# Low-rank attention on one core: 64-row products in pairs, and the sums of key tiles shared out anew

## Chip, core and metric

The kernel runs on one core of a Trainium2 chip. The metric is the device time of one execution in microseconds, median of several runs.

## What is computed

Six layers on x of shape 8 x 1024 x 128, each on the layer norm of the running sum: a low-rank expert layer, attention in windows of 64 with 16 heads, the expert layer again, a linear layer on values rounded to a 6-bit grid, low-rank attention, and the linear layer again. The change is in low-rank attention. Cut to what matters:

```python
# per batch b: y = layernorm(x[b]); y @ W_DKV, y @ W_KR, y @ W_DQ give 32 numbers each
q = concatenate([q_c, q_r], -1)             # 8 heads, 128 + 32
k = concatenate([k_c, k_r], -1)
scores = einsum('bhsd,bhtd->bhst', q, k) * scale
attn = softmax(scores, -1)                  # 1024 queries x 1024 keys
o = einsum('bhst,bhtd->bhsd', attn, v_c)
x = x + (o.transpose(...).reshape(...) @ W_O + b_O)
```

The products of weight matrices are taken beforehand, so that keys and queries of a head meet in 64 numbers (KR), the keys are the same for all heads of a batch, and values have 32 numbers (DC).

## The kernel before

There are 8 batches of 8 heads, 64 heads u in all, each with 8 key tiles of 128 keys (NT) and 1024 queries. A step g = 8u + t is one key tile of one head; 512 steps in all. For each engine the program runs over the same list of steps (`plan_m`, made by `low_rank_plan`), and each engine executes what it has in that order and waits on semaphores.

Precision is kept by splitting: keys and queries are held as a rounded high part and the low rest, both in a format that TensorE takes in one pass. `key_hl` has the high part in rows 0 to 63 and the low part in rows 64 to 127, `q_hi` has the high part of the queries twice, `key_h1` the high keys and a row of ones, `q_low` the low queries and a row with the shift of the exponent.

In step g TensorE (`pe_low_rank`) does, for each half of the columns:
- `pe_row_scores` (L1825) for a tile 14 steps ahead: 128 queries against 512 keys, one product of 128 rows. VectorE takes the maximum of each row (`dve_row_max`, L1833). When a head's maxima are there, `dve_row_top`, `pool_shift` and `sync_move_shift` make the shift of the exponent and move it by DMA into its row. The banks are 4, 5, 6 in turn (`ROW_BANKS`), shared with the totals;
- `pe_key_scores` (L1878 and L1882) for tile g: two products of 512 columns, 128 and 65 rows deep, into one bank. The banks are 0, 1, 2 in turn (`K_BANKS`), so half n waits for the exponential of half n - 3. ScalarE takes the exponentials (`act_exponentials`, L1893) into `prob1`, which has room for eight tiles.

Then come the low-rank items that the plan has put there (`pe_low_part`: queries of a later head, and once a batch the turned input, keys, constants, values, output projection and the last linear layer), which share bank 7: an item waits until the one before it in the bank has been taken away. On odd groups of four steps (g mod 8 = 3) and even ones (g mod 8 = 7) follows `pe_weigh`: four tiles are weighed with the values (L1936, 32 rows of output at four column places), and for g mod 8 = 3 the totals of a head are made first (L1929). For the totals GpSimd has added up tiles 0 to 6 of the head (`pool_sum`, L1904 and L1907), and TensorE adds that sum and tile 7. VectorE inverts the totals (`dve_invert_totals`, L1946) and scales the result (`dve_normalise`), and SP moves it (`sync_move_head`).

A wait stands in each engine's own program ahead of the instruction that needs it, and everything behind it on that engine stands too.

Of the kernel before, what the change touches and what calls it, by code (L numbers as in the profile page):

```python
# [225 lines left out]
PIPELINE = 16  # L226
# [3 lines left out]
def low_rank_plan():  # L230
# [34 lines left out]
    while g < NT * U + 26 or running or waiting:  # L265
        early, late = [], []
# [7 lines left out]
        if r == (12 if b < B else 7) and 1 <= b <= B:  # L274
            waiting[0:0] = [("proj", b - 1, i) for i in range(2)]
# [11 lines left out]
        if item is None and waiting and (g % 2 == 0 or g >= NT * U):  # L287
            item = waiting.pop(0)
        if item:
            run = begin(item, FINAL_BANKS.get((item[0], item[2]), 7) if item[1] == B - 1 else 7)  # L290
            late.append((tuple(run[:3]), 1))
            running.append(run)
        steps.append((g, early, late))
# [4 lines left out]
def build_program(nc, x_in, w128, w_mla, w_out_window, w33, w1, consts, out):  # L298
    ctx = ExitStack()
    with ctx:  # L300
# [37 lines left out]
        both_parts = sb("both_parts", [P, DC], F32R)  # L338
# [71 lines left out]
        w_query = sb("w_query", [QR + 2, NH, 2 * KR], F32R, low)  # L410
# [6 lines left out]
        key_hl = sb("key_hl", [P, 2, T], F32R, low)  # L417
        key_h1 = sb("key_h1", [KR + 1, 2, T], F32R, low)
# [3 lines left out]
        q_hi = sb("q_hi", [P, Q_BUFS, T], F32R, low)  # L422
        q_low = sb("q_low", [KR + 1, Q_BUFS, T], F32R, low)
        amax1 = sb("amax", [P, 2, NT, 2], F32, low)
        shift = sb("shift", [P, 2, 2, 4], F32, low)
        shift_cols = sb("shift_cols", [P, 2, 4], F32R, low)
# [1009 lines left out]
        def pool_layers(e):  # L1436
            for i in range(B + 1):
# [5 lines left out]
                if i == 3:  # L1443
                    e.wait_ge(*dequant.at(("c", i - 2)))
                    e.memset(key_h1[KR:KR + 1, :, :].bitcast(F32), 1.0).then_inc(*set_low.up("key row"))
                    e.wait_ge(*set_low.at("key row"))
# [30 lines left out]
        key_h1_done = signal("key_high_copied")  # L1477
# [5 lines left out]
        shift_moved = [(new_sem(f"shift_row_{k}_first_half"), new_sem(f"shift_row_{k}_last_half")) for k in range(Q_BUFS)]  # L1483

        def shift_ready(u, i):
            return shift_moved[u % Q_BUFS][i], 64 * (u // Q_BUFS + 1)
# [145 lines left out]
        def pe_low_part(e, item, j, before, part):  # L1632
# [5 lines left out]
            if kind == "query":  # L1638
                b, h = divmod(a, NH)
                e.wait_ge(*cq_ready.at((b, 1)))  # L1640
                e.matmul(bank(j), w_query[:, h, :], cq[:, b % 2, sl], start=True, stop=True,  # L1641
# [41 lines left out]
            else:  # L1683
                e.wait_ge(*mla_built.at("both"))
                e.wait_ge(*keys_done.at((a, 1)))
                for t in range(NT):
# [572 lines left out]
```

## Time and profile before

| | us |
|---|---|
| median of 3 runs | 1807.89 |
| lowest, highest | 1807.46, 1809.03 |
| span of the profiled execution | 1812.5 |
| TensorE busy | 1670.4 (92%) |
| VectorE busy | 1393.8 (77%) |
| GpSimd busy | 1177.3 (65%) |
| ScalarE busy | 1137.5 (63%) |
| mean granted TensorE clock | 0.967 |

The profiled execution is its own run; its time is taken here as its span, 4.6 us above the median. The layers before low-rank attention fill the first third of the span; the low-rank stage runs from about 610 to 1780 us. In it the profile shows few names: key and row products, exponentials, row maxima, sums, totals and weighing. Busy time on TensorE counts overlapping records once, and a product's record is longer than its share of the engine, since the next one starts before it ends.

### The profile page before, as it was taken

The numbers are of one execution on the slowest core, as the hardware profiler recorded it, in microseconds if no ns is written. First come the engines' busy times: TensorE is split into PE (matmuls) and PEld (weight loads), VectorE is DVE, ScalarE is ACT, GpSimd is POOL, SyncE is SP. The second block draws the span as 40 slices with busy tenths as digits, with TensorE's granted clock in tenths as the row PEclk, the third lists the DMA queues.
The fourth block names the chain that finished last, engine by engine and source line by source line (L and its number), as shares of the span: only waits on it lengthen the run. The fifth ranks groups of instructions, "written<-read, shape, count | busy, mean of one in ns | idle before, by whom it ended". The sixth has DMA issues, their size and how long they took to land.

```text
span 1812.5 us, 39662 instructions
## 1 busy us (share of the span) xinstructions
PE 1670.4 (92%) x15057; PEld 1223.0 (67%) x15057; DVE 1393.8 (77%) x2976; ACT 1137.5 (63%) x2222; POOL 1177.3 (65%) x909
## 2 busy tenths in 40 slices
PE   4679999999877899999999999999999999999995
PEld 4557777777766567666766766766676677677674
DVE  5557777766597888878888888888887888888862
ACT  5447777777676466666666666666656666665662
POOL 4300111000066498898898988989889898898892
PEclk9889999999887899999999999999999999999997
DMA  4556666654000000000000000001001000100101
GB/s 123 136 140 156 162 156 159 164 136 116 29 1 1 1 10 8 10 8 10 7 13 16 10 8 19 11 7 22 7 10 19 8 10 7 22 7 10 19 10 30
DMA packets 198677, 81.47 MB, mean 45 GB/s; under 512 B 152553, under 2 KB 177493, under 8 KB 198357
## 3 DMA queue, kind: packets, MB, share of 16 engines
q1 hardware_dynamic: 198484, 78.93, 19.5%
q8 instruction: 119, 1.95, 0.5%
q14 instruction: 74, 0.60, 0.1%
HBM read 39.79 MB, written 29.88 MB: 38 GB/s over the span
## 4 chain that ended last, share of the span: by engine, by line
PE 54%; DVE 11%; POOL 2%; issue 1%; ACT 1%; DMA 0%; SPq 0%; POOLq 0%; ACTq 0%
PE pair L1825 12%; PE pair L1878 11%; PE pair L1882 11%; PE pair L1936 10%; DVE amax L1833 4%; PE pair L1929 4%; PE pair L1650 2%; DVE o_inv L1946 1%; PE pair L1641 1%; DVE stats L485 1%; POOL w_mix L1907 1%; PE pair L1664 1%; DVE q_low L1754 1%; DVE cq L1765 1%; DVE key_hl L1768 1%
## 5 line engine op out<-in xcount | busy, mean ns | idle before, releaser
L1893 ACT ACTIVATE prob<-pair 128x512 f32<-128x512 f32 x1024 | 604.4, 597 | 422.2 <-PE pair L1882 359.6
L1833 DVE TENSOR_REDUCE amax<-pair 128x1 f32<-128x512 f32 x1024 | 670.3, 682 | 133.9 <-PE pair L1825 131.8
L1825 PE MATMUL pair<-key_hl,q_hi 128*128 128x512 f32 x1024 | 437.8, 430 | 11.2 <-DVE amax L1833 7.1
L1878 PE MATMUL pair<-q_hi,key_hl 128*128 128x512 f32 x1024 | 405.2, 396 | 2.6 <-ACT prob L1893 2.6
L1882 PE MATMUL pair<-q_low,key_h 65*128 65x512 f32 x1024 | 406.0, 396 | 0.0
L1907 POOL TENSOR_TENSOR w_mix<-w_mix,prob 128x1024 f32<-128x1024 f32 x160 | 382.3, 2389 | 25.2 <-ACT prob L1893 8.5
L1907 POOL TENSOR_TENSOR Wm<-Wm,prob 128x1024 f32<-128x1024 f32 x155 | 369.6, 2384 | 20.8 <-ACT prob L1893 4.1
L520 POOL TENSOR_SCALAR veps<-mv 128x8 f32<-128x8 f32 x47 | 11.4, 243 | 452.6 <-DVE mv L493 451.2
L1825 PEld LDWEIGHTS pair<-key_hl,q_hi 128*128 128x128 f32 x1024 | 196.1, 192 | 115.9 <-issue 51.0
L1936 PE MATMUL pair<-prob,values 128*32 128x256 f32 x4096 | 247.2, 382 | 0.0
L1186 DVE TENSOR_REDUCE mx_neg<-pair 128x4 f32<-128x512 f32 x256 | 164.9, 687 | 94.8 <-PE pair L1090 94.1
L1878 PEld LDWEIGHTS pair<-q_hi,key_hl 128*128 128x128 f32 x1024 | 195.5, 191 | 44.3 <-ACT prob L1893 9.4
L1882 PEld LDWEIGHTS pair<-q_low,key_h 65*128 65x128 f32 x1024 | 192.5, 188 | 44.6
L1936 PEld LDWEIGHTS pair<-prob,values 128*32 128x32 f32 x4096 | 127.5, 110 | 100.9 <-issue 25.0
L1136 ACT ACTIVATE yT<-pair 128x512 f32<-128x512 f32 x256 | 138.6, 593 | 72.3 <-PE pair L1042 70.3
L1946 DVE RECIPROCAL o_inv<-pair 128x256 f32<-128x256 f32 x64 | 112.5, 1758 | 59.8 <-PE pair L1929 59.8
L542 ACT ACTIVATE y<-x,mean_neg,rstd 128x128 f32<-128x128 f32 x336 | 137.7, 485 | 19.0 <-POOL mean_neg L528 18.9
L1090 PE MATMUL pair<-keys,queries 64*128 64x128 f32 x1024 | 100.5, 317 | 0.0
L1042 PE MATMUL pair<-queries,keys 64*128 64x128 f32 x1024 | 97.0, 309 | 0.0
L1702 ACT ACTIVATE q_hi<-pair 128x512 fp32r<-128x512 f32 x128 | 75.7, 591 | 20.0 <-PE pair L1641 20.0
L1754 DVE TENSOR_TENSOR q_low<-pair,q_hi 64x512 fp32r<-64x512 f32 x128 | 86.3, 675 | 2.2 <-ACT q_hi L1702 2.2
L1090 PEld LDWEIGHTS pair<-keys,queries 64*128 64x128 f32 x1024 | 82.7, 199 | 3.7
(209 smaller groups left out, 2232.8 us busy)
## 6 DMA issues: line engine op xcount, KB each, us to landing
rows_mem<-once SPq DMA_DIRECT2D x128, 128.0 KB, 2.0
queries<-rows_mem SPq DMA_DIRECT2D x64, 256.0 KB, 4.5
keys<-rows_mem SPq DMA_DIRECT2D x16, 1024.0 KB, 7.1
rows_mem<-once SPq DMA_DIRECT2D x128, 64.0 KB, 1.9
q_low<-shift_cols SPq DMA_DIRECT2D x512, 0.5 KB, 2.0
yT<-o_norm SPq DMA_DIRECT2D x256, 32.0 KB, 1.9
x<-x_dram SPq DMA_DIRECT2D x8, 512.0 KB, 7.3
out_dram<-x SPq DMA_DIRECT2D x7, 512.0 KB, 3.4
```

What stands on the lines that cost most here:

```text
L542: ins = e.activation(y_of(stage, b)[:, t, :], x[:, b * NT + t, :], ACT.Identity, bias=mean_neg[:, k, t:t + 1], scale=rstd[:, k, t:t + 1])
L1090: ins = e.matmul(bank(S_BANKS[r])[:, q * P:(q + 1) * P], queries[rows, hb % QUERY_BUFS, q, m].rearrange("p s w -> p (s w)"), keys[rows, b ...
L1136: e.activation(pT[:, u % P_TURNED].rearrange("p q k -> p (q k)"), key_row_bank(*divmod(u, 2)), ACT.Exp).then_inc(*exps.up(u))
L1186: e.tensor_reduce(mx_neg[:, hb % 2, r, :, m], bank(S_BANKS[r]).rearrange("p (q k) -> p q k", q=QUADS), AX_X, ALU.max, negate=True).then_in ...
L1825: e.matmul(row_bank(("row", r, i)), q_hi[:, k, t * P:(t + 1) * P], key_hl[:, b % 2, i * HALF:(i + 1) * HALF], start=True, stop=True, skip_ ...
L1833: e.tensor_reduce(amax1[:, u % 2, t, i:i + 1], row_bank(("row", r, i)), AX_X, ALU.max).then_inc(*row_maxed.up((r, i)))
L1878: e.matmul(bank(j), key_hl[:, b % 2, ks], q_hi[:, k, sl], start=True, stop=False, skip_group_check=True)
L1882: e.matmul(bank(j), key_h1[:, b % 2, ks], q_low[:, k, sl], start=False, stop=True, skip_group_check=True).then_inc(*key_scored.up((g, half)))
L1893: e.activation(prob1[:, g % P_BUFS, half * HALF:(half + 1) * HALF], bank(K_BANKS[(2 * g + half) % 3]), ACT.Exp, scale=SCALE1).then_inc(*ke ...
L1907: e.tensor_tensor(into, into, p, ALU.add).then_inc(*summed_keys.up(g))
L1936: ins = e.matmul(bank(PVB)[q * DC:(q + 1) * DC, 0:QUARTER], values[:, b % 2, t, :], prob1[:, g % P_BUFS, q * QUARTER:(q + 1) * QUARTER], s ...
L1946: e.reciprocal(o_inv[:, u % 2, :], row_bank(("total", u, 0))[:, 0:QUARTER]).then_inc(*o_inverse.up(u))
```

## The change

- Keys and queries: `key_high` has the high keys in rows 0 to 63 and again in 64 to 127, `key_low` the low keys twice. `q_hi` and `q_low` have the first 512 queries in rows 0 to 63 and the last 512 in rows 64 to 127, and so does the new `q_shift`, of which only rows 0 and 64 are not zero; `ones_shift` is all ones. A head's queries come from two products into one bank, then one copy and one subtraction of 128 rows.
- Row scores are made of the high parts alone, by two products of 64 rows, one in each half of the rows, into two banks.
- Key scores of a tile are four such pairs: high keys with high queries, low keys with high queries, high keys with low queries, ones with the shift. Both sides begin together, after the waits for both banks.
- GpSimd adds up six tiles of a head instead of seven; two go to the totals directly.
- The plan: the queries come at g mod 8 = 7, other items only at g mod 8 = 3, one ahead of the weighing and, unless it or the next is a key product (`low`), one behind it.
- The shift is made once a head and moved by eight DMAs in a row.

```diff
     def regular(g):
-        for i in range(2):
-            u, rest = divmod(g + 16 - 4 * i, NT)
-            if rest == 0 and 0 <= u < U:
-                return "query", u, i
-        return None
+        u, rest = divmod(g + PIPELINE, NT)
+        return ("query", u, 0) if rest == 0 and 0 <= u < U else None
...
-        if item is None and waiting and (g % 2 == 0 or g >= NT * U):
+        if item is None and waiting and (g % NT == 3 or g >= NT * U):
             item = waiting.pop(0)
...
+        if g % NT == 3 and 0 <= g < NT * U and waiting and item[0] != "low" and waiting[0][0] != "low":
+            run = begin(waiting.pop(0))
+            after.append((tuple(run[:3]), 1))
+            running.append(run)
...
-                e.matmul(bank(j), w_query[:, h, :], cq[:, b % 2, sl], start=True, stop=True,
+                e.matmul(bank(j), w_query[:, h, KR:3 * KR], cq[:, b % 2, 0:HALF], start=True, stop=False,
+                         skip_group_check=True)
+                e.matmul(bank(j), w_query[:, h, 0:2 * KR], cq[:, b % 2, HALF:T], start=False, stop=True,
                          skip_group_check=True).then_inc(*query_done.up((a, i)))
...
                 for t in range(NT):
-                    ins = e.matmul(bank(j)[:, t * DC:(t + 1) * DC], key_hl[:, a % 2, t * P:(t + 1) * P], both_parts[:, :],
-                                   start=True, stop=True, skip_group_check=True)
+                    for part in (key_high, key_low):
+                        ins = e.matmul(bank(j)[:, t * DC:(t + 1) * DC], part[:, a % 2, t * P:(t + 1) * P],
+                                       first_dims[:, :], start=part is key_high, stop=part is key_low,
+                                       skip_group_check=True)
...
+        def pe_row_scores(e, r):
+
+            u, t, half = row_tiles(r)
             b, k = u // NH, u % Q_BUFS
...
+            for side in range(2):
+                row_bank_free(e, ("row", r, side))
+            for side in range(2):
+                rows = slice(side * KR, (side + 1) * KR)
+                e.matmul(row_bank(("row", r, side)), q_hi[rows, k, t * P:(t + 1) * P],
+                         key_high[rows, b % 2, half * HALF:(half + 1) * HALF], start=True, stop=True,
+                         skip_group_check=True).then_inc(*row_scored.up((r, side)))
...
-            if n >= 3:
-                e.wait_ge(*key_exp.at(divmod(n - 3, 2)))
-            e.matmul(bank(j), key_hl[:, b % 2, ks], q_hi[:, k, sl], start=True, stop=False, skip_group_check=True)
...
+            banks = [bank(K_BANKS[(2 * g + side) % 3]) for side in range(2)]
...
+            for side in range(2):
+                if 2 * g + side >= 3:
+                    e.wait_ge(*key_exp.at(divmod(2 * g + side - 3, 2)))
+            for part in range(4):
...
+                for side in range(2):
+                    rows = slice(side * KR, (side + 1) * KR)
+                    weights = ones_shift[rows, :] if part == 3 else (key_low if part == 1 else key_high)[rows, b % 2, ks]
+                    moving = (q_hi, q_hi, q_low, q_shift)[part][rows, k, :]
+                    ins = e.matmul(banks[side], weights, moving, start=part == 0, stop=part == 3, skip_group_check=True)
+                    if part == 3:
+                        ins.then_inc(*key_scored.up((g, side)))
...
                 if u < B * NH - 1:
-                    e.wait_ge(*summed_keys.at(NT * u + 6))
-                    parts = prob1[:, (NT * u + 7) % P_BUFS, :], key_sum[u % 2]
+                    e.wait_ge(*summed_keys.at(NT * u + 5))
+                    parts = *(prob1[:, (NT * u + t) % P_BUFS, :] for t in (6, 7)), key_sum[u % 2]
...
-                for half in range(2):
-                    if 0 <= g + ROW_LEAD < total:
-                        pe_row_scores(e, g + ROW_LEAD, half)
-                    if 0 <= g < total:
-                        pe_key_scores(e, g, half)
+                if 0 <= g + ROW_LEAD < total:
+                    pe_row_scores(e, g + ROW_LEAD)
+                if 0 <= g < total:
+                    pe_key_scores(e, g)
                 for (item, j, before), part in late:
                     pe_low_part(e, item, j, before, part)
                 if g % 4 == 3 and 0 <= g // 4 - 1 < total // 4:
                     pe_weigh(e, g // 4 - 1)
+                for (item, j, before), part in after:
+                    pe_low_part(e, item, j, before, part)
...
-                if (g - 1) % NT in range(1, 7) and 0 <= g - 1 < total - NT:
+                if (g - 1) % NT in range(1, 6) and 0 <= g - 1 < total - NT:
                     pool_sum(e, g - 1)
```

## Rows read from the trace of the kernel before

**Rows 1.** Of the page, part 1: busy us of each engine (share), instructions.

```profile
PE 1670.4 (92%) x15057; PEld 1223.0 (67%) x15057; DVE 1393.8 (77%) x2976; ACT 1137.5 (63%) x2222; POOL 1177.3 (65%) x909
```

**Rows 2.** Stretch, length, busy of five engines, granted clock, DMA share, GB/s.

```profile
1200.00:1400.00 200.00, 195.57 (x1507) 137.23 (x1506) 166.35 (x310) 125.56 (x230) 179.97 (x126) 1.00 0.09 14
```

**Rows 3.** Timeline of one head: start us, duration, instruction [idle before].

```profile
1206.44 0.39 PE L1882 MATMUL pair<-q_low,key_h 65*128 65x512 f32 x1
...
1206.87 1.30 ACT L1893 ACTIVATE prob<-pair 128x512 f32<-128x512 f32 x2 [3.02 <-PE pair L1882]
...
1207.14 0.40 PE L1882 MATMUL pair<-q_low,key_h 65*128 65x512 f32 x1
```

**Rows 4.** The same timeline, totals and weighing after step 3 of a head.

```profile
1202.83 0.39 PE L1882 MATMUL pair<-q_low,key_h 65*128 65x512 f32 x1
...
1203.14 0.64 PE L1929 MATMUL pair<-prob,ones_col 128*32 128x256 f32 x8
...
1203.60 0.61 PE L1929 MATMUL pair<-Wm,ones_col 128*32 128x256 f32 x8
...
1205.87 0.19 PEld L1825 LDWEIGHTS pair<-key_hl,q_hi 128*128 128x128 f32 x1 [0.41 <-issue]
```

**Rows 5.** The same timeline, a wait for ScalarE and a weighing without totals.

```profile
1211.24 1.05 ACT L1893 ACTIVATE prob<-pair 128x512 f32<-128x512 f32 x2
...
1211.87 0.50 PE L1878 MATMUL pair<-q_hi,key_hl 128*128 128x512 f32 x1 [0.36 <-ACT prob L1893]
...
1212.21 0.40 PE L1882 MATMUL pair<-q_low,key_h 65*128 65x512 f32 x1
...
1214.40 0.50 PE L1825 MATMUL pair<-key_hl,q_hi 128*128 128x512 f32 x1
...
1215.67 0.40 PE L1882 MATMUL pair<-q_low,key_h 65*128 65x512 f32 x1
```

**Rows 6.** Timeline of TensorE in the window stage, with pairs of 64-row products.

```profile
301.87 0.39 PE L1085 MATMUL pair<-mask_bf,both_rows 64*128 64x512 bf16 x2 [0.17 <-DVE mx_neg L1186]
301.90 0.74 PE L1090 MATMUL pair<-keys,queries 64*128 64x128 f32 x8
302.49 0.39 PE L1035 MATMUL pair<-both_rows,mask_bf 64*128 64x512 bf16 x2
...
303.20 1.07 PE L1061 MATMUL pair<-yT,vals 128*17 128x128 f32 x32
```

**Rows 7.** Lines, 640 to 1740 us: xcount | busy, mean ns | idle.

```profile
L1833 DVE TENSOR_REDUCE amax<-pair 128x1 f32<-128x512 f32 x957 | 627.5, 682 | 123.4 <-PE pair L1825 121.3
L1893 ACT ACTIVATE prob<-pair 128x512 f32<-128x512 f32 x958 | 567.6, 597 | 391.3 <-PE pair L1882 330.8 <-POOL Wm L1904 6.1
...
L1907 POOL TENSOR_TENSOR w_mix<-w_mix,prob 128x1024 f32<-128x1024 f32 x150 | 358.5, 2390 | 23.9 <-ACT prob L1893 8.5
...
L1946 DVE RECIPROCAL o_inv<-pair 128x256 f32<-128x256 f32 x60 | 105.5, 1758 | 36.1 <-PE pair L1929 36.1
```

**Rows 8.** Timeline of TensorE in the last steps.

```profile
1769.82 0.74 PE L1929 MATMUL pair<-prob,ones_col 128*32 128x256 f32 x8 [1.76 <-POOL w_mix L1907]
```

**Rows 9.** Timeline of the head above, ScalarE normalising four tiles.

```profile
1209.70 1.63 ACT L542 ACTIVATE y<-x,mean_neg,rstd 128x128 f32<-128x128 f32 x4
```

**Rows 10.** Who waited for whom, 640 to 1740 us: total us, times, longest.

```profile
PEld pair L1825 <- DVE amax L1833: 14.0, 35, 1.3
...
PEld pair L1878 <- ACT prob L1893: 6.5, 13, 0.8
```

**Rows 11.** TensorE by stretch: stretch, length, busy, granted clock, DMA share, GB/s.

```profile
139.50:375.00 235.50, 220.37 (x3250) 0.99 0.63 155
603.80:613.90 10.10, 9.40 (x20) 0.54 0.06 0
```

**Rows 12.** Timeline of the first key tile, at the lower clock.

```profile
611.19 0.63 PE L1882 MATMUL pair<-q_low,key_h 65*128 65x512 f32 x1
...
611.62 0.63 PE L1825 MATMUL pair<-key_hl,q_hi 128*128 128x512 f32 x1
```

More of the change, by code:

```diff
@@ L225 @@
 ROW_LEAD = 14
-PIPELINE = 16
+PIPELINE = 17
 Q_BUFS, P_BUFS = 3, 8
@@ L265, in low_rank_plan @@
     while g < NT * U + 26 or running or waiting:
-        early, late = [], []
+        early, late, after = [], [], []
         b, r = divmod(g, NT * NH)
@@ L1801, in build_program @@
         row_uses = []
-        for g, early, late in plan_m:
+        for g, early, late, after in plan_m:
             if 0 <= g + ROW_LEAD < total:
@@ new lines, in dve_row_max, with dve_row_top @@
+        def dve_row_max(e, r, side):
+            u, t, half = row_tiles(r)
+            e.wait_ge(*row_scored.at((r, side)))
+            if u >= 2:
+                e.wait_ge(*row_topped.at(u - 2))
+            e.tensor_reduce(amax1[:, u % 2, NT // 2 * side + t, half:half + 1], row_bank(("row", r, side)), AX_X,
+                            ALU.max).then_inc(*row_maxed.up((r, side)))
+        def dve_row_top(e, u):
+            e.wait_ge(*row_maxed.at((NT * u + NT - 1, 1)))
+            if u:
+                e.wait_ge(*shift_steps.at((u - 1, 1)))
+            e.tensor_reduce(shift[:, 0, :], amax1[:, u % 2, :, :], AX_X, ALU.max).then_inc(*row_topped.up(u))
@@ new lines, in pool_shift @@
+        def pool_shift(e, u):
+            b, h = divmod(u, NH)
+            top, mc = (shift[:, n, :] for n in range(2))
+            c = ccol[:, b % 2, :, h]
+            e.wait_ge(*row_topped.at(u))
+            e.wait_ge(*const_ready.at(b))
+            if u:
+                e.wait_ge(*shift_steps.at((u - 1, 2)))
+            e.tensor_tensor(mc, top, c, ALU.add).then_inc(*shift_steps.up((u, 1)))
+            e.wait_ge(*shift_steps.at((u, 1)))
+            if u:
+                e.wait_ge(*shift_ready(u - 1))
+            e.tensor_tensor(shift_cols[:, :], c, mc, ALU.subtract).then_inc(*shift_steps.up((u, 2)))
@@ new lines, in sync_move_shift @@
+        def sync_move_shift(e, u):
+            e.wait_ge(*shift_steps.at((u, 2)))
+            queries_free(e, u)
+            if u == 0:
+                e.wait_ge(*set_low.at("shift rows"))
+            for t in range(NT):
+                side, n = divmod(t, NT // 2)
+                e.dma_start(q_shift[side * KR:side * KR + 1, u % Q_BUFS, n * P:(n + 1) * P].bitcast(F32).rearrange(
+                    "o (p t) -> o p t", t=1), shift_cols[:, t:t + 1].bitcast(F32)).then_inc(
+                    shift_moved[u % Q_BUFS], 16)
@@ L1993, in pe_low_rank @@
             e.wait_ge(*x_dve.at(("c", B - 2)))
-            for g, early, late in plan_m:
+            for g, early, late, after in plan_m:
                 if g == CONST_AT:
@@ L2056, in dve_low_rank @@
         def dve_low_rank(e):
-            for g, early, late in plan_m:
+            for g, early, late, after in plan_m:
                 if g == CONST_AT + 1:
@@ L2077, in pool_low_rank @@
         def pool_low_rank(e):
-            for g, early, late in plan_m:
+            for g, early, late, after in plan_m:
                 for (item, j, before), part in early:
@@ L2151, in sync @@
                 if u < B * NH:
-                    for i in range(2):
-                        sync_move_shift(e, u, i)
+                    sync_move_shift(e, u)
                 if u >= 2:
```

156 lines of the change are left out of this document (60 added, 96 removed).

## The prediction

> **What bounds the kernel now.** I read the page first, then the busy times by stretch, then the order of instructions of one head, then who waited for whom. The changed code is the low-rank stage. In the page TensorE is busy 92% of a span of 1812.5 us [rows 1], and in a stretch in the middle of the stage 195.57 of 200 us at a granted clock of 1.00, with VectorE at 166, GpSimd at 180 and ScalarE at 126 [rows 2]. A TensorE record overlaps its neighbour, so busy time alone doesn't say how dense it is: the order of instructions does. There, 512-column products start 0.233 us apart (three passes from 1206.44 to 1207.14) [rows 3]. A step, one of a head's eight key tiles, is six such passes: 1.40 us, and TensorE goes straight on to the next one. It is paced by its own passes.
>
> A head is eight steps. After the last key product of step 3 come totals and weighing (4.31 us from that product to the last one of the next step, 1202.83 to 1207.14) [rows 3, 4]; after step 7 comes weighing alone (3.46 us, 1212.21 to 1215.67) [rows 5]. The other six intervals are 1.40 us.
>
> **What the change saves.** The row product becomes one pair of 64-row products instead of two passes. If the members of a pair run side by side, a step has five passes instead of six. The trace has such pairs in the window stage: two 64x512 and eight 64x128 products, alternating in row halves, take 0.62 us from 301.87 to 302.49 [rows 6]. One after another their 2048 columns would need 0.85 us at 2.4 GHz, and side by side 0.43; with eight loads of 128-column weights on the way, 0.62 fits only side by side. I price a pair like one pass, 0.233. The step then has 5 x 0.233 = 1.17 us of TensorE work.
>
> The Trainium skill, TensorE: Matmul & The Clock Gate, Part 3, says the same, a pack costs one product and about 4 ns for each tile after the first. The same skill, TensorEngine Tiling (Array Packing), PSUM Bottleneck, warns that tiling speeds up the array and not the emptying of PSUM. The next part is what that warning would mean here, worked out from rows.
>
> **What the change adds: a closed ring.** Key scores keep three banks. Before, each half is finished by two passes, alone, and a half waits for the exponential three halves back. After, both sides of tile g are worked on together and both finish in the last of four pairs; tile g needs two banks, and the second is the one that side 0 of tile g-1 filled. So no key product of tile g starts before the exponential of (g-1, side 0) ends, and that one can't start before all of tile g-1 is done. Only the row pair, 0.233 us, stands between on TensorE. The ring, from last key pair to last key pair:
> - last product starts to exponential starts: 0.43 (1206.44 to 1206.87) [rows 3];
> - one exponential: 0.60 [rows 7];
> - its end to the waiting product: 0.03 (1211.24 + 0.60 to 1211.87) [rows 5];
> - the first product after a wait to the next: 0.34 (1211.87 to 1212.21) [rows 5], as its weights load in the open;
> - two more pairs: 0.47.
>
> Sum 1.87 us against 1.40. Everything else fits inside: two exponentials (2 x 0.60 on ScalarE), two row maxima (2 x 0.68 on VectorE) [rows 7]. **Six ordinary intervals: 6 x 0.47 = +2.82 us a head.** Bound below: if the weights of the first pair load early, 0.11 less each, +2.16.
>
> **The interval with the query** (step 7). The two query products move here, into one bank. Before: 3.46 + 2 x 0.233 elsewhere = 3.93. After: 2.19 from last key product past the weighing (1212.21 to 1214.40) [rows 5], + 0.47 query, + a change between array shapes, + row pair and four key pairs 0.34 + 0.70. For that change the rows of the window stage give 0.09: the same block takes 0.62 before 64-row work and 0.71 (302.49 to 303.20) before 32-column work [rows 6]; the other end is the 0.41 that the weight load stands idle after a weighing [rows 4]. I take 0.09, since a queue that is full hides most of it: 3.79, so **-0.14**. The exponential is over long before the weighing ends.
>
> **The interval with totals** (step 3). A third tile goes through the totals: eight more products, 0.46 (1203.14 to 1203.60) [rows 4]. After: 3.04 + 0.46 + 1.04 = 4.54 against 4.31, **+0.23**. What it buys is one addition of 2.39 us on GpSimd [rows 7]. It is worth nothing on the path: in the steady stretch GpSimd is not what TensorE waits for; the one long wait of that kind is 1.76 us, once, in the last steps [rows 8].
>
> **Smaller terms, per head.** ScalarE is now on the ring, so its other work ahead of an exponential counts where it exceeds the 0.67 us that ScalarE has free in a step. Normalising takes 16 activations per batch of eight heads, four in 1.63 us [rows 9]: at most 0.8 a head, at least 0; much of it meets a weighing, I take +0.20. Low-rank items put behind the weighing share bank 7 with the one ahead of it. For three a batch (second halves of projection and product, and the values) the bank is emptied by VectorE, in order behind the 1.76 us reciprocal [rows 7]: 0 to 1.2 us each, I take 0.5, so +0.20. Eight more value products and the shape changes around the items: 0 to 0.4, +0.10. The waits that TensorE had for the row maxima and exponentials, 14.0 + 6.5 us over 60 heads [rows 10], go: -0.30. VectorE's single query-low part and single top, and the copy to the upper key rows on ScalarE, all lie beside other work. The eight shift DMAs now go together, after step 7 of the row products, with seven tiles' time until they are needed; nothing queues behind them on SP but the heads' moves, needed later still.
>
> **Sum.** 2.82 - 0.14 + 0.23 + 0.20 + 0.20 + 0.10 - 0.30 = +3.11 us a head, x 64 = +199. Once: the last 14 steps have no row products, so their TensorE work was less while the ring is the same, another 0.47 in ten of them, +5; the wait for GpSimd in the last steps goes, -2; a larger fill by GpSimd (128 x 1536 in one of the layer stages, bounds 0 and 4 from 2.39 us per 1024 [rows 7]) +2. Together +204: 1812.5 + 204 = 2016.5 for a profiled execution. That one lies 4.6 us above the median of the runs, so 2012.
>
> **Rivals.**
> (A) *The exponential is hidden and TensorE's passes count.* Then a step saves one pass: 8 x 0.233 = 1.87 a head less 0.46 for totals and 0.09, so -1.3 x 64 = -84: 1724. It decides at one point: the ring must close within 1.40 us. For it: TensorE is the bound now. Against: 0.43 + 0.60 + 0.70 is 1.73 even if both hand-overs and the weight load cost nothing. 5%.
> (B) *The pairs don't overlap.* Each of four key pairs is two passes: the ring gets 4 x 0.233 longer, 2.80, and the two other intervals 5 x 0.233 each: (6 x 0.93 + 2 x 1.17) x 64 = +507 on top: about 2520. The blocks of the window stage speak against [rows 6]. 4%.
> (C) *The granted clock falls.* TensorE now stands still about 0.4 us in every ordinary step. In the row-product prelude, where it waited for VectorE each time, the granted clock was 0.54 on average [rows 11]; passes were 0.43 apart there (611.19 to 611.62) [rows 12]. At that level the ring is 0.43 + 0.23 (a product of 0.63 instead of 0.40) + 0.60 + 0.03 + 0.43 x 3 = 2.58. If three of six ordinary steps run so: 3 x 0.71 x 64 = +136: 2148. Against: the window stage, full of short waits too, kept 0.99 over 235 us [rows 11], and the ring is broken twice a head by 2 to 3 us of solid weighing. 12%.
> (D) *No measurable change*, ring and savings cancelling: needs an ordinary interval of about 1.35 us, since the terms other than the ring add up to +0.29 a head. 1%.
>
> **How the numbers follow.** The forecast, 2012, has 78%. Its own bounds: without the exposed weight load (-0.66 a head) and the three small terms (-0.50) it is 2012 - 74 = 1938; with all normalising exposed (+0.60) and 0.41 for two shape changes a head (+0.64) it is 2012 + 79 = 2091. These bounds hold nearly all of it. The range 1937 to 2095 leaves out A, B, D and most of C. What a measurement can tell from no change is about 0.2%. Faster by over that: A, 5%. Within: 1%. Slower: 94%.
>
> **What would show it.** In the profile after, key products of a tile stand as four pairs 0.23 us apart; a wait of about 0.4 us stands ahead of most first key products, ended by the exponential; ordinary steps repeat every 1.87 us; a head grows by about 3.1 us. The busy shares of all engines fall. Wrong would be: pair members one after another (B), granted clock under 0.95 in the steady stretch (C), steps of 1.2 us with no wait for ScalarE (A). If steps are 1.87 but the total is off, the small terms or the two long intervals were mis-sized.

## The result

The changed kernel takes 2073.23 us (median of 4 runs, 2070.34 to 2081.53) against 1808.46 us for the kernel before: a ratio of 1.145, 95% interval 1.141 to 1.149. It is slower by 265 us; the forecast was 2012, slower by 204, with a range of 1937 to 2095. The profiled execution has a span of 2079.7 us.

The profile after, parts 1, 4 and 5 of its page, beside [rows 1]:

```profile
PE 1749.3 (84%) x17673; PEld 1176.5 (57%) x17673; DVE 1335.8 (64%) x2865; ACT 1077.8 (52%) x2158; POOL 1007.0 (48%) x719
...
PE 57%; ACT 14%; DVE 12%; issue 6%; SPq 5%; DMA 4%; POOL 3%; POOLq 0%; ACTq 0%; DVEq 0%
...
L1918 ACT ACTIVATE prob<-pair 128x512 f32<-128x512 f32 x1024 | 555.9, 595 | 709.4 <-PE pair L1906 707.2
...
L1906 PE MATMUL pair<-q_hi,key_high 64*128 64x512 f32 x1024 | 244.9, 463 | 153.4 <-ACT prob L1918 153.1
```

TensorE, 92% busy before, is 84% busy, and all other engines are busy by more than a tenth less. The chain that ended last has 14% of ScalarE in it. The exponentials (L1918) take the same 595 ns each as in [rows 7], but TensorE now stands idle for them: 153.1 us ahead of L1906, the first product of a tile.

The stretch that answers to [rows 2], busy time of the engines in the same order:

```profile
1200.00:1400.00 200.00, 172.44 (x1582) 106.24 (x1580) 129.05 (x242) 94.22 (x177) 121.07 (x74) 0.97 0.07 11
```

The timeline of two ordinary steps, the query step and the weighing of one head, which answers to [rows 3] and [rows 5]; "x2" is a pair, and a PEld line is the load of the weights:

```profile
1310.15 0.42 PE L1906 MATMUL pair<-q_shift,ones_shift 64*128 64x512 f32 x2
...
1310.38 0.42 PE L1843 MATMUL pair<-key_high,q_hi 64*128 64x512 f32 x2
1310.58 1.09 ACT L1918 ACTIVATE prob<-pair 128x512 f32<-128x512 f32 x2 [0.85 <-PE pair L1906]
...
1311.29 0.21 PEld L1906 LDWEIGHTS pair<-q_hi,key_high 64*128 64x128 f32 x2 [0.92 <-ACT prob L1918]
1311.32 0.50 PE L1906 MATMUL pair<-q_hi,key_high 64*128 64x512 f32 x2 [0.52 <-ACT prob L1918]
...
1311.63 0.42 PE L1906 MATMUL pair<-q_hi,key_low 64*128 64x512 f32 x2
...
1312.09 0.42 PE L1906 MATMUL pair<-q_shift,ones_shift 64*128 64x512 f32 x2
...
1312.45 0.50 PE L1645 MATMUL pair<-cq,w_query 98*128 98x512 f32 x1
...
1312.79 0.39 PE L1647 MATMUL pair<-cq,w_query 98*128 98x512 f32 x1
...
1313.11 1.93 PE L1961 MATMUL pair<-prob,values 128*32 128x256 f32 x32
...
1314.97 0.51 PE L1843 MATMUL pair<-key_high,q_hi 64*128 64x512 f32 x2
```

What is to be seen: both members of a pair go together, and pairs that find their weights loaded follow each other after 0.23 us. The last pair of a tile starts at 1310.15. The exponential starts at 1310.58, 0.43 later. The next tile's first weight load stands idle for 0.92 us and goes at 1311.29, when ScalarE has side 0 done; its last pair starts at 1312.09. The step is 1.94 us, with one row pair of 0.23 inside TensorE's wait.

To see the whole stage, I took the start of the last key product of each of the 512 tiles from the timeline and averaged the eight intervals of a head. Interval 3 holds totals, weighing and most items, interval 7 the other weighing:

| us | 0 | 1 | 2 | 3 | 4 | 5 | 6 | 7 | head |
|---|---|---|---|---|---|---|---|---|---|
| before, mean | 1.67 | 1.39 | 2.06 | 4.35 | 1.67 | 1.46 | 2.21 | 3.45 | 18.3 |
| after, mean | 1.95 | 1.95 | 1.94 | 6.20 | 1.98 | 2.22 | 2.09 | 4.00 | 22.3 |
| after, median | 1.95 | 1.95 | 1.94 | 5.72 | 1.95 | 1.95 | 1.94 | 3.92 | |

A head costs 4.07 us more (18.26 and 22.33 before rounding). The first tile's last product comes 7.5 us later than before (619.98 against 612.47); the 34.5 us behind the last one are the same in both.

### The profile page after: what moved, and what is told of

Same layout as the page of the kernel before. It is cut to its first block, busy times and chain, and to the rows that moved or that the text cites. A ratio compares the mean times of both kernels' runs of the same rounds, so it can differ in the third digit from the quotient of the medians.

```text
span 2079.7 us, 45103 instructions
## 1 busy us (share of the span) xinstructions
PE 1749.3 (84%) x17673; PEld 1176.5 (57%) x17673; DVE 1335.8 (64%) x2865; ACT 1077.8 (52%) x2158; POOL 1007.0 (48%) x719
## 4 chain that ended last, share of the span: by engine, by line
PE 57%; ACT 14%; DVE 12%; issue 6%; SPq 5%; DMA 4%; POOL 3%; POOLq 0%; ACTq 0%; DVEq 0%
PE pair L1906 24%; ACT prob L1918 9%; PE pair L1961 8%; PE pair L1954 5%; PE pair L1843 3%; DVE amax L1852 3%; DMA keys<-rows_mem 3%; ACT y L545 2%; DVE o_inv L1971 2%; PE pair L1656 2%; SPq L955 1%; PE pair L1645 1%; SPq L935 1%; PE pair L1064 1%; SPq L936 1%
## 5 line engine op out<-in xcount | busy, mean ns | idle before, releaser
L1918 ACT ACTIVATE prob<-pair 128x512 f32<-128x512 f32 x1024 | 555.9, 595 | 709.4 <-PE pair L1906 707.2
L1906 PE MATMUL pair<-q_hi,key_high 64*128 64x512 f32 x1024 | 244.9, 463 | 153.4 <-ACT prob L1918 153.1
L1843 PE MATMUL pair<-key_high,q_hi 64*128 64x512 f32 x1024 | 250.2, 469 | 49.1 <-DVE amax L1852 47.7
L1906 PEld LDWEIGHTS pair<-q_hi,key_high 64*128 64x128 f32 x1024 | 108.4, 187 | 272.9 <-ACT prob L1918 270.2
L1906 PE MATMUL pair<-q_shift,ones_shift 64*128 64x512 f32 x1024 | 216.4, 399 | 0.0
L1906 PE MATMUL pair<-q_low,key_high 64*128 64x512 f32 x1024 | 216.0, 398 | 0.0
L1906 PE MATMUL pair<-q_hi,key_low 64*128 64x512 f32 x1024 | 215.5, 397 | 0.0
L1843 PEld LDWEIGHTS pair<-key_high,q_hi 64*128 64x128 f32 x1024 | 109.4, 189 | 174.3 <-issue 87.2
L1906 PEld LDWEIGHTS pair<-q_shift,ones_shift 64*128 64x128 f32 x1024 | 108.7, 188 | 12.8
L1906 PEld LDWEIGHTS pair<-q_low,key_high 64*128 64x128 f32 x1024 | 108.9, 189 | 12.5
L1906 PEld LDWEIGHTS pair<-q_hi,key_low 64*128 64x128 f32 x1024 | 110.8, 191 | 5.7
```

Of the source, the lines that this page charges most:

```text
L1843: e.matmul(row_bank(("row", r, side)), q_hi[rows, k, t * P:(t + 1) * P], key_high[rows, b % 2, half * HALF:(half + 1) * HALF], start=True, ...
L1906: ins = e.matmul(banks[side], weights, moving, start=part == 0, stop=part == 3, skip_group_check=True)
L1918: e.activation(prob1[:, g % P_BUFS, half * HALF:(half + 1) * HALF], bank(K_BANKS[(2 * g + half) % 3]), ACT.Exp, scale=SCALE1).then_inc(*ke ...
```

## The experiments

The theory: an ordinary step is bound by the ring from a tile's last pair over the exponential to the next tile's first pair, and nothing that TensorE itself has to do. The rivals: pairs, or changes of the array's shape between products, cost more than they look; VectorE's maxima hold the steps; GpSimd needed the relief. Each ratio is to the kernel before, run beside it.

### Open the ring by order alone, and cut the exponential

**e1_skew**: the same products, with side 1 two pairs behind side 0, and ScalarE in that order.

```diff
-            for part in range(4):
...
-                for side in range(2):
...
+            for part in range(4):
+                if g < total:
+                    product(g, 0, part)
+                if part < 2 and g:
+                    product(g - 1, 1, part + 2)
+                elif part >= 2 and g < total:
+                    product(g, 1, part - 2)
...
-            for half in range(2):
+            for g, half in ((g - 1, 1), (g, 0)):
```

> The changed kernel with one thing altered, the order inside the pairs: side 1 of a key tile runs two pairs behind side 0, so a pair holds part p of side 0 of tile g and part p+2 of side 1 of tile g-1 (or p-2 of the same tile), and ScalarE takes side 1 of tile g-1 just before side 0 of tile g. Number of products, pairs, exponentials and banks as before it. Ring theory: the step has two rings of two pairs each instead of one of four; each is 0.43 + 0.60 + 0.15 from last product to the product that may follow, and one more pair, 0.31, so an ordinary step takes 1.49 us where the changed kernel shows 1.94. Six a head and 64 heads give -173 us: 1900, between 1885 and 1930 if row maxima now bind now and then. Theory that pairs cost more than one pass or that TensorE's shape changes make the loss: nothing in the work has changed, so the time stays at 2073.

Measured: 1950.03 us, ratio 1.078 (1.076 to 1.080): 123 us less than the changed kernel for the same work. The timeline of an ordinary step:

```profile
1305.14 0.39 PE L1903 MATMUL pair<-q_shift,ones_shift 64*128 64x512 f32 x1
1305.17 0.39 PE L1903 MATMUL pair<-q_hi,key_low 64*128 64x512 f32 x1
...
1305.38 0.50 PE L1843 MATMUL pair<-key_high,q_hi 64*128 64x512 f32 x2
...
1305.77 0.49 PE L1903 MATMUL pair<-q_hi,key_high 64*128 64x512 f32 x1
...
1305.77 0.49 PE L1903 MATMUL pair<-q_low,key_high 64*128 64x512 f32 x1
...
1306.56 0.39 PE L1903 MATMUL pair<-q_shift,ones_shift 64*128 64x512 f32 x1
```

Pairs now hold one product of a tile's end and one of a tile's start. From 1305.14 to 1306.56 the step is 1.42 us instead of 1.94, better than the 1.49 expected; two half rings that run beside each other would give this, but no run takes them apart. So neither the pairs themselves nor a change of shape made the 1.94. The total fell by 123 us where 173 was expected. Two intervals lag most: the one behind the query step stayed at 1.97 by the median, and the one that the table further down calls 5 is 3.6 at two heads of each batch, those with low products. The cause of the first stands in the same kernel's trace:

```profile
1310.51 0.60 ACT L1711 ACTIVATE q_hi<-pair 128x512 fp32r<-128x512 f32 x1 [2.89 <-PE pair L1903]
```

ScalarE's copy of the queries (L1711) waits for the last product that uses the old buffer, and that product now comes one step later; the exponential of the tile stands behind the copy. In e10 and e11 below, where the copy comes later, this interval is 1.42.

**e3_half_exp_after** and **e4_half_exp_before**: the same cut in both kernels, which leaves out half of the softmax weights. (Both also clear two tiles of `prob1` once, ahead of the stage, which the diff below leaves out.)

```diff
-                e.activation(prob1[:, g % P_BUFS, half * HALF:(half + 1) * HALF], bank(K_BANKS[(2 * g + half) % 3]),
+                e.activation(prob1[:, g % P_BUFS, half * HALF:half * HALF + QUARTER],
+                             bank(K_BANKS[(2 * g + half) % 3])[:, 0:QUARTER],
```

> The changed kernel with each exponential taken over the first 256 of its 512 columns (half of the weights of the softmax are left out; the rest of the buffers holds old numbers). An exponential should take about 0.4 us instead of 0.60. Ring theory: every ordinary step is shorter by the same 0.2 us, 0.2 x 384 = -77 us: about 1996. If TensorE's own work is the bound: 2073, less than 10 us off.

> The same cut in the kernel before: each exponential over 256 of 512 columns. There TensorE goes on while ScalarE works, so both theories expect next to nothing: 1808, at most 10 us less from the waits for exponentials that the trace shows (6.5 us). It is the control for the run of the changed kernel.

Measured: 2015.1 us (ratio 1.112, 1.109 to 1.115), 58 less than the changed kernel; and in the kernel before 1810.22, ratio 1.000 (0.9985 to 1.0008). One line of the groups from 700 to 1700 us of each, after's variant first, and two ordinary steps of that variant:

```profile
L1920 ACT ACTIVATE prob<-pair 128x256 f32<-128x256 f32 x743 | 244.5, 381 | 620.5 <-PE pair L1908 620.5
```

```profile
L1895 ACT ACTIVATE prob<-pair 128x256 f32<-128x256 f32 x868 | 329.0, 383 | 525.4 <-PE pair L1884 518.2
```

```profile
1305.31 0.42 PE L1908 MATMUL pair<-q_shift,ones_shift 64*128 64x512 f32 x2
...
1306.27 0.51 PE L1908 MATMUL pair<-q_hi,key_high 64*128 64x512 f32 x2 [0.31 <-ACT prob L1920]
...
1307.04 0.44 PE L1908 MATMUL pair<-q_shift,ones_shift 64*128 64x512 f32 x2
```

An exponential takes 381 ns instead of 595, 0.21 less, and the step from 1305.31 to 1307.04 is 1.73, also 0.21 less. What is taken from ScalarE comes off the step in full in one kernel and not at all in the other, where ScalarE has the same work. This settles the ring. Six steps of 64 heads at 0.21 would be 81 us, and the median run shows 58: intervals 4 to 6, in which other work stands too, fall by less, and the granted clock of three of the four runs is 0.948 to 0.950, where the changed kernel has 0.953 to 0.960.

### The hand-over

**e2_one_wait**: only the later of the two waits ahead of a tile is kept.

```diff
-            for side in range(2):
-                if 2 * g + side >= 3:
-                    e.wait_ge(*key_exp.at(divmod(2 * g + side - 3, 2)))
+            if g:
+                e.wait_ge(*key_exp.at((g - 1, 0)))
```

> The changed kernel waits twice ahead of a key tile, for the exponentials three and two halves back; the second implies the first, so the first is left out here. The changed kernel shows 0.12 to 0.15 us from the end of the exponential to the first key product, where 0.03 was expected. If the second wait instruction makes that, the ordinary step falls by about 0.1 and the time by 0.1 x 384 = 38 us to 2035. If the hand-over takes that long anyway, 2073.

Measured: 2051.44 us, ratio 1.133 (1.130 to 1.136), 22 less. The ordinary step is 1.88 by the median of all heads, 0.06 less. From the end of the exponential to the second key pair it takes 0.45 us in the changed kernel (0.15 to the first pair, 0.31 to the next) and 0.39 here (0.05 and 0.33), by the median; the forecast had 0.37. So of the 0.08 that this stretch is longer than forecast, 0.06 is the extra wait, which is satisfied long before. The rest is open.

### The sums on GpSimd

**e5_seven_after** undoes this part in the changed kernel; **e6_six_before** makes it alone in the kernel before. The diff is that of e6; e5 is the same the other way round.

```diff
-                    if before % NT < NT - 1:
+                    if before % NT < NT - 2:
...
-                    e.wait_ge(*summed_keys.at(NT * u + 6))
-                    parts = prob1[:, (NT * u + 7) % P_BUFS, :], key_sum[u % 2]
+                    e.wait_ge(*summed_keys.at(NT * u + 5))
+                    parts = *(prob1[:, (NT * u + t) % P_BUFS, :] for t in (6, 7)), key_sum[u % 2]
...
-                if (g - 1) % NT in range(1, 7) and 0 <= g - 1 < total - NT:
+                if (g - 1) % NT in range(1, 6) and 0 <= g - 1 < total - NT:
```

> The changed kernel with one part undone: GpSimd adds up seven key tiles again, TensorE's totals take the sum and tile 7. The interval with totals should lose the eight products of the third part, 0.46 us, and GpSimd, busy 48% in the changed kernel, has room for one more addition of 2.37 us a head. 0.46 x 63 = -29 us: 2044. Theory that GpSimd needed the relief: no gain, 2073 or more.

> The kernel before with this one part of the change alone: GpSimd adds up six tiles, two go to the totals. TensorE is the bound there, so the 0.46 us a head are added: +0.46 x 63 = +29 us, 1838; if the waits for the sums that the trace shows (about 2 us in the steady stretch, 1.8 at the end) go, 3 less. Theory that GpSimd at 90% was holding TensorE back: 1809 or less.

Measured: 2051.24 (ratio 1.131, 1.127 to 1.135), 22 less; and 1829.46 (ratio 1.010, 1.008 to 1.012), 18 more. The interval with totals moves by 0.43 and 0.42 us by the median (5.72 to 5.29, 4.33 to 4.75). The part is a loss in either kernel. In the kernel before GpSimd was busy 90% of the time in [rows 2], and taking work from it gained only what the totals of the first head and of the last but one [rows 8] had waited for the sum: these two intervals went from 5.81 to 4.75 and from 7.40 to 4.30, about 5 us together once the 0.42 that each pays is counted.

### VectorE's queue

**e7_drain_first**: the item ahead of the weighing is taken out of bank 7 before the reciprocal.

```diff
-                    dve_low_part(e, item, j, before, part)
+                    if (item, part) not in drained:
+                        dve_low_part(e, item, j, before, part)
...
                 if t == 0 and 0 <= u < B * NH:
+                    if g < total:
+                        for (item, j, before), part in late:
+                            if item[0] in ("proj", "const", "product"):
+                                drained.add((item, 2))
+                                dve_low_part(e, item, j, before, 2)
                     dve_invert_totals(e, u)
```

> The changed kernel with one thing reordered on VectorE: the result of a low-rank item ahead of the weighing (output projection, constants, last product) is taken out of bank 7 before the reciprocal of the totals instead of after it. In the changed kernel the item behind the weighing waits for it, 8.3 + 7.1 + 5.0 us in total at the weight loads. If that order is what costs, these waits go: -20 to -25 us, 2050. If the wait only moves to the maxima of the next row pair, 2073.

**e8_no_reciprocal**: a copy of the totals takes the reciprocal's place, so the division of the softmax is left out.

```diff
-            e.reciprocal(o_inv[:, u % 2, :], row_bank(("total", u, 0))[:, 0:QUARTER]).then_inc(*o_inverse.up(u))
+            e.tensor_copy(o_inv[:, u % 2, :], row_bank(("total", u, 0))[:, 0:QUARTER]).then_inc(*o_inverse.up(u))
```

> The changed kernel with the reciprocal of the totals (1.76 us on VectorE) replaced by a copy of the same size (about 0.4 us); the division of the softmax is left out. In the changed kernel the weight loads of row pairs wait 62 us for row maxima and those of items another 20 us for VectorE. If VectorE's backlog after the reciprocal makes both, most of it goes: -60 to -80 us, 2000. If they come from other work of VectorE (statistics, rounding scales), only the 20 us go: 2050. The ring itself must stay at 1.94.

Measured: 2067.43 (ratio 1.142, 1.139 to 1.145) and 2062.56 (1.140, 1.136 to 1.143). That is 6 and 11 us less than the changed kernel, where each expectation had 20 or more if VectorE's order or the reciprocal made the waits, and both intervals overlap its own, 1.141 to 1.149. Who waited for whom, 700 to 1960 us, total us, times, longest, changed kernel first and then e8_no_reciprocal:

```profile
PEld pair L1906 <- ACT prob L1918: 228.2, 294, 1.5
...
PEld pair L1843 <- DVE amax L1852: 61.6, 105, 2.0
...
PEld pair L1656 <- DVE x L1769: 8.3, 7, 1.2
```

```profile
PEld pair L1906 <- ACT prob L1918: 232.5, 302, 1.5
...
PEld pair L1843 <- DVE amax L1852: 59.8, 104, 2.0
...
PEld pair L1656 <- issue: 5.5, 14, 0.4
```

The waits of items for VectorE (L1656 is the projection) are gone in e8, down to the 0.4 us a load needs anyway, and the interval with totals falls from 6.20 to 5.97 (e7) and 5.99 (e8) by the mean. But the waits of row pairs for maxima are what they were: the reciprocal doesn't make them. The largest single part, 24 of the 61.6 us in twelve waits, comes at the two low products of each batch, as here in the changed kernel's own trace:

```profile
1259.12 0.75 DVE L1774 SCALAR_TENSOR_TENSOR cq<-pair,Wt,cq 32x512 fp32r<-32x512 f32 x1
...
1259.90 1.50 DVE L1778 SCALAR_TENSOR_TENSOR key_low<-pair,Wt,key_high 64x512 fp32r<-64x512 f32 x2
...
1261.43 2.65 DVE L1852 TENSOR_REDUCE amax<-pair 128x1 f32<-128x512 f32 x4
...
1262.27 0.54 PE L1843 MATMUL pair<-key_high,q_hi 64*128 64x512 f32 x2 [1.61 <-DVE amax L1852]
...
1263.41 0.68 PE L1906 MATMUL pair<-q_low,key_high 64*128 64x512 f32 x2
...
1263.84 0.68 PE L1906 MATMUL pair<-q_shift,ones_shift 64*128 64x512 f32 x2
```

L1774 and L1778 are VectorE's three steps on a low product, 2.25 us together, one of them new. They stand ahead of the maxima; the row pair waits 1.61 us. Behind it pairs are 0.43 us apart, and the granted clock was 0.50 there. (In the rows: stretch, length, TensorE's busy time and instructions, granted clock, DMA share, GB/s.)

```profile
1250.00:1262.00 12.00, 9.81 (x96) 1.00 0.10 13
1262.90:1265.30 2.40, 2.10 (x12) 0.50 0.03 7
1266.00:1278.00 12.00, 10.67 (x101) 1.00 0.03 0
```

There are twelve such stretches at half the clock between 640 us and the last tile, 51 us together; the kernel before has one, of 3.4 us. Six of the twelve stand behind a wait of 1.6 us for a maximum and two behind one of 1.1 us for ScalarE. The other four have no wait above 0.3 us in the 6 us ahead of them. There the sixteen value products of 32 columns (eight before the change) had just run, the last of them at 1282.59 in this example:

```profile
1278.00:1282.80 4.80, 4.57 (x70) 1.00 0.06 4
1283.20:1286.40 3.20, 2.86 (x15) 0.50 0.12 30
...
1282.59 0.26 PE L1695 MATMUL pair<-first_dims,key_low 128*128 128x32 f32 x1
...
1283.14 0.64 PE L1906 MATMUL pair<-q_hi,key_high 64*128 64x512 f32 x2
1283.57 0.64 PE L1906 MATMUL pair<-q_hi,key_low 64*128 64x512 f32 x2
```

At the same places of other batches, with the same waits and products, the clock stays at 1.00, so neither always brings it down. Compared with those, the 25 intervals that the stretches touch are 20 us longer in sum: an estimate of what the clock costs here, 0.3 us a head.

**e9_low_later** puts those three steps behind the two maxima of their step.

```diff
                 for (item, j, before), part in early:
-                    dve_low_part(e, item, j, before, part)
+                    if item[0] != "low" or g < 0:
+                        dve_low_part(e, item, j, before, part)
...
+                for (item, j, before), part in early:
+                    if item[0] == "low" and g >= 0:
+                        dve_low_part(e, item, j, before, part)
```

> The changed kernel with VectorE's work on a low product (three steps of 0.75 us, the third new: the second copy of the low keys) put behind the two row maxima of its step instead of ahead of them. In the changed kernel TensorE waits 1.6 us for the maxima there, twice a batch, and the granted clock halves for 3.4 us behind it. If that queue is the cause, the waits of row pairs for maxima fall from 62 us to under 45, and with the clock it gives 2 x 7 x (1.6 + 0.7) = -32 us at most, -15 at least: 2050. If the maxima are late for another reason, 2073.

Measured: 2071.53 (ratio 1.145, 1.141 to 1.148): no gain, where 15 to 32 us were expected. The waits for maxima fall from 61.6 to 52.4 us. Interval 5 falls from 2.22 to 1.95, and interval 6 rises from 2.09 to 2.22: VectorE has 1.94 - 1.29 = 0.65 us to spare in a step, 2.25 us of work overrun it wherever they stand, and most of the wait moves one step on.

### Everything mended

**e10_all_mended** takes e1, e5, e7 and e9 together, and ScalarE's copy of the queries goes behind the exponentials of its step. What is new:

```diff
                 for (item, j, before), part in early:
-                    act_low_part(e, item, j, before, part)
+                    if item[0] != "query" or g < 0:
+                        act_low_part(e, item, j, before, part)
                 if 0 <= g <= total:
                     act_exponentials(e, g)
+                for (item, j, before), part in early:
+                    if item[0] == "query" and g >= 0:
+                        act_low_part(e, item, j, before, part)
```

> The changed kernel with what the runs so far point to, together: side 1 two pairs behind side 0 (1950), seven tiles on GpSimd (-22), items drained ahead of the reciprocal (-6), low products behind the maxima (-15 to -30), and ScalarE's copy of the queries behind the exponentials of its step: in the run with the skew it waited for the last key product of side 1, now a step later, and held the exponential back by about 0.5 us once a head (-30). Sum 1950 - 22 - 6 - 20 - 30 = 1872, between 1850 and 1890. Ring theory says that it stays above the kernel before, since an ordinary step is 1.42 us against 1.40 and the pair's spared pass is not seen. Theory that pairs are a gain once the ring is open: under 1808.

Measured: 1967.78 (ratio 1.087, 1.083 to 1.092), worse than e1 alone, though the sum had promised 1872. Interval 1 is 2.56 us, where e1 has 1.47. The timeline there:

```profile
1318.02 0.61 ACT L1711 ACTIVATE q_hi<-pair 128x512 fp32r<-128x512 f32 x1
...
1318.66 0.69 DVE L1763 TENSOR_TENSOR q_low<-pair,q_hi 128x512 fp32r<-128x512 f32 x1 [0.79 <-ACT q_hi L1711]
1319.27 1.28 DVE L1852 TENSOR_REDUCE amax<-pair 128x1 f32<-128x512 f32 x2
...
1320.09 0.50 PE L1843 MATMUL pair<-key_high,q_hi 64*128 64x512 f32 x2 [1.17 <-DVE amax L1852]
```

The copy is done at 1318.63; VectorE waited 0.79 us for it with the maxima behind, and the row pair at 1320.09 waited 1.17. A copy moved out of one engine's way stood in another's.

**e11_all_mended_b** moves VectorE's part of the queries behind the maxima too and takes e9 back. **e12_mended_half_exp** is that kernel with the half exponentials of e3, and leaves out what e3 does. The diff is e11 against e10, in VectorE's loop:

```diff
-                    if (item, part) not in drained and (item[0] != "low" or g < 0):
+                    if (item, part) not in drained and (item[0] != "query" or g < 0):
...
-                    if item[0] == "low" and g >= 0:
+                    if item[0] == "query" and g >= 0:
```

> As the kernel with all mended, but VectorE's part of the queries also goes behind the row maxima of its step, and its part of the low products is back ahead of them. In the run with all mended the step after the copy had VectorE wait 0.79 us for it ahead of the maxima, and TensorE 1.17 us for those: the interval grew from 1.42 to 2.59 us once a head. With that gone: (2.56 - 1.45) x 63 = -70 us, 1968 - 70 = 1898; if the low products' wait in the seventh and eighth interval goes as well, -40 more: 1860 to 1900. Ring theory: above 1808 all the same. Theory that an open ring makes pairs a gain: under 1808.

> The same kernel with exponentials over 256 of 512 columns (half of the softmax weights left out). If the three banks still bind the ordinary step at 1.42, it falls by two thirds of the 0.2 us an exponential loses (two bank uses a step share three banks), until the two row maxima of 1.29 us bind: about 1.30, so -0.12 x 384 = -45 us. If TensorE or VectorE already binds at 1.42: no change.

Measured: 1922.1 (ratio 1.062, 1.059 to 1.065) and 1902.74 (1.052, 1.049 to 1.054). The means of the eight intervals:

| us | 0 | 1 | 2 | 3 | 4 | 5 | 6 | 7 | head |
|---|---|---|---|---|---|---|---|---|---|
| e1_skew | 1.95 | 1.47 | 1.51 | 6.16 | 1.57 | 1.99 | 1.65 | 3.91 | 20.2 |
| e10_all_mended | 1.42 | 2.56 | 1.62 | 5.53 | 1.53 | 1.52 | 2.16 | 4.22 | 20.6 |
| e11_all_mended_b | 1.42 | 1.51 | 2.11 | 5.67 | 1.53 | 1.99 | 1.66 | 3.90 | 19.8 |
| e12_mended_half_exp | 1.35 | 1.39 | 2.19 | 5.69 | 1.47 | 1.99 | 1.56 | 3.91 | 19.6 |

e11 misses its range of 1860 to 1900. Interval 1 falls as expected, but interval 2 rises from 1.62 to 2.11: VectorE's 0.69 us for the low queries (L1763) now stand ahead of the next step's maxima, and its row pair's weights wait 0.78 us. In e11 weight loads of row pairs wait for maxima 133.3 us, more than in any kernel above:

```profile
PEld pair L1843 <- DVE amax L1852: 133.3, 227, 2.5
...
PEld pair L1903 <- ACT prob L1926: 43.0, 113, 2.0
```

The same two rows of e12, whose lines are numbered two higher; both are from 700 to 1840 us:

```profile
PEld pair L1845 <- DVE amax L1854: 151.7, 226, 2.6
...
PEld pair L1905 <- ACT prob L1928: 15.9, 15, 1.5
```

With 381 ns exponentials the free steps fall only from 1.42 to 1.34 by the median, close to the 1.29 us of two maxima. Key pairs now hardly wait for ScalarE, and row pairs wait for VectorE as often as before. So behind the ring stands VectorE, at about 1.3, and TensorE's own 1.17 is never reached. This is read from the waits: no run made the maxima shorter, and two thirds of 0.21 off the 1.42 would be 1.28 by the banks too.

None of these kernels comes near the one before. e11, the fastest of those that leave nothing out, takes 1.5 us more a head (19.8 against 18.3): its free steps gain nothing (1.42 against 1.40), and row pairs wait for maxima 2.3 us a head, where they had waited 0.23 [rows 10].

## Why the prediction was right, and where it was off

**The direction and the mechanism were right.** The forecast ring of 1.87 us is the ordinary step of 1.94, e3 and e4 show that ScalarE's time is on it one to one, and e1 that its closedness, not the work, makes it. Rival A (the spared pass counts) falls with the steps; B (no overlap) with pairs 0.23 us apart. C happened in small: the granted clock is 0.98 over the stage, where the kernel before had 1.00, and the twelve stretches at half the clock cost about 20 us by the estimate above. They stand at a few places of a batch, behind longer waits or the value products, and not behind the 0.5 us that TensorE waits in every ordinary step.

**The size was 61 us short.** The result lies in the range, but that is partly luck: its upper end was worked out from normalising and from changes of shape, and what made most of the miss (a longer ring, VectorE's queue and the clock) is not in it. By the terms of the sum, per head:

| term | forecast | measured |
|---|---|---|
| ring, six intervals | +2.82 | +3.24 (6 x (1.94 - 1.40)) |
| query interval | -0.14 | -0.01 (3.92 - 3.93) |
| totals interval without items | +0.23 | +0.24 (4.55 at heads with no item, against 4.31) |
| everything else | +0.20 | +0.6 (the rest of 4.07) |

- *The ring*: the hand-over from ScalarE to the waiting product was taken as 0.03 from [rows 5]; it is 0.15 here (1310.58 + 0.595 to 1311.32). The restart was a little cheaper, 0.31 for 0.34. Of the 0.08 that remain, 0.06 is the extra wait (e2).
- *The query interval*: the change of shape was taken as 0.09 from [rows 6]. A query product follows the last key pair after 0.36 instead of 0.23, so 0.13, and the second query product comes 0.34 behind the first, since its weights load in the open; that 0.11 was not in the sum.
- *Everything else* hides the step that failed: "VectorE's single query-low part and single top ... all lie beside other work", and with it -0.30 for waits that would go. They didn't go, they grew: those for maxima from 14.0 us over 60 heads [rows 10], 0.23 a head, to 61.6 over 57, 1.08 a head. Not all of that is time, since short ones run beside the ring's own wait, but intervals 4 to 6 are 0.44 us above the 1.95 in sum, where the low products and other work of VectorE stand. The sum counted VectorE's load over a step (2 x 0.68 in 1.87) and left out that the low products' work, with a new third part, stands in the same queue ahead of the maxima. The bank-7 wait, taken as +0.20, is about that by the trace (6.20 against 5.97 in e7) and less by the run time, which shows 6 us, within its noise. And about 0.3 of the 0.6 is the clock, which the sum had at nothing; part of it lies in the same intervals, so the two don't add up one by one.
- *Once*: the first tile comes 7.5 us later where +2 was forecast. It comes at 614.0 to 622.3 in the changed kernel and its ten variants, and at 603.0 to 612.5 in the kernel before and its two. From 560 us to that tile TensorE was at half the clock for 46 to 51 us in the former and for 19 to 30 in the latter. How much of the delay is the clock and how much the fill wasn't tested.

That the relief of GpSimd is worth nothing was right, in both kernels, but for the two waits that e6 removes; the forecast had the later one, at -2.

The Trainium skill (TensorEngine Tiling (Array Packing), PSUM Bottleneck) says that tiling makes the array faster and not the emptying of PSUM, which may then set the pace. These runs agree in part: the array's part of the step fell from 1.40 to 1.17 us (five pairs of 0.233), and the wait for a bank to be emptied set the time at 1.94. But the emptying itself was not too slow: with the same exponentials in another order the step was 1.42 (e1).

## What to carry to other kernels

Two products side by side also finish side by side. Count the banks: with three, the next pair needs one of the two just filled, and its wait is a full product, a full evacuation and two hand-overs; running the sides half a tile apart gave back 123 us for the same work. Before an engine is made faster, add up the ring through its banks and ask which engine comes second: here VectorE's two maxima, 1.29 us, would have left at most 0.1 of the 0.23 us that was to be won. And in an in-order queue the load over a step says little; what stands ahead of the instruction that others wait for is what counts, as e10 showed once more.

## What the runs showed of the hardware

- With one wait in place of two ahead of a tile, of which the first had long been satisfied, a step was 0.06 us shorter (e2).
- 64-row pairs of 512 columns repeat every 0.23 us (1311.63 to 1312.09 for two), the pace of one 128-row product [rows 3], with two weight loads of 0.19 each in that time.
- From a 64-row pair to a 98-row product takes 0.36 (1312.09 to 1312.45) instead of 0.23.
- In a stage that was otherwise dense, waits of 1.1 to 1.6 us were followed in some batches and not in others by a stretch at half the granted clock, with pairs 0.43 apart. So were sixteen products of 32 columns, 0.11 us apart, without any wait above 0.3 us.
- An exponential of 256 columns takes 381 ns and one of 512 takes 595, so 167 ns of it don't depend on the columns, if the rest grows in proportion to them. Two in a row start 0.50 us apart (1.09 for the two together).
